# A three-stage kernel: scratch columns for the squares, the prologue's orders rewritten, a rounding put ahead of a search round, and the flags in another PSUM bank

## The chip, the cores and the metric

The kernel runs on one core of a Trainium2 chip. The metric is the device time of one execution in microseconds (us), lower being better. TensorE (PE) multiplies matrices, VectorE (DVE), ScalarE (ACT) and GpSimd (POOL) work elementwise, SyncE (SP) only issues DMAs here; each works through its own queue in order, and semaphores order them against each other.

## The reference

2048 rows of 512 numbers go through three residual stages: x + 0.5 ffn(norm(x)), then x + attn(norm(x)), then x + 0.5 ffn(norm(x)).

```python
def ffn(x, A, B, Wr):                      # stages 1 and 3
    scores = x @ Wr.T                      # 64 of them a row
    top_vals, top_idx = top_k(scores, 16)
    G = scatter(softmax(top_vals))         # 0 elsewhere
    h = einsum('nd,krd->nkr', x, A)        # 64 groups of 16
    return einsum('nkr,kdr->nd', h * G[:, :, None], B) * 2.0

def attn(x, w_gate, w_up, w_down):         # stage 2, inner width 1376
    s = silu(x @ w_gate.T)
    s[the 688 smallest of |s| in each row] = 0
    return (s * (x @ w_up.T)) @ w_down.T
```

All is float32, so each product is made of three float16 products: both factors are split into a high and a low half, and hi*hi, lo*hi and hi*lo are summed.

## The kernel before

There are 16 tiles of 128 rows. A tile passes stage 1 (`experts(1, t)`: 64 scores and 1024 columns of A; `choose`, `exps`, `route` and `apply_route`: the 16 largest and their weights; `p_to_hi` and `p_to_lo`: the product's halves; `turn_p`: both halves transposed by DMA; `combine`: the product with B; `add_ffn`), stage 2 and stage 3, which is as stage 1. In stage 2 `gates`, `tanh` and `silu` make the gate, `magnitude` its absolute values and their sum, and `aim` a first guess at the threshold. Seven rounds follow: `count` on ScalarE counts how many magnitudes lie above the threshold (a sign with a sum), and `search` on GpSimd moves the threshold by four small instructions (L407 to L411). `select` on VectorE takes the exact value from the last few, and writes a flag if the threshold was too far off; `sum_flags` sums it over the partitions with a matmul of ones (L599), and `check` reads the sum and runs a slow exact search if it isn't zero. `mask`, `ups`, `gated`, `v_to_hi`, `v_to_lo`, `turn_v`, `down` and `add_down` finish the stage.

All orders are written out by hand, one list for each engine. Eleven steady tiles (`tile(d)`, `FULL` = 11) work on stage 3 of tile d, on the second half of stage 2 of d+1, on the first half of d+2, and on stage 1 of d+5. Ahead of them lies the prologue, which loads and prepares the weights, and behind them a tail.

PSUM has eight banks: `DOWN` = 0 takes the product of `down` (and in the prologue turned rows and sums of squares), `COMB` = 1 that of `combine`, 2 to 4 the wide products, 5 and 6 A's, and `SCORE` = 7 the scores; before, the flags' sum lies in column 64 of bank 7. So `sum_flags` waits until the scores ahead of it are read, and the next `experts` waits for `flag_read`.

A weight matrix is prepared in pieces. It lands in the stage `mem`; `square` on ScalarE (L681) writes its squares in bfloat16 to scratch columns; `norms` on TensorE (L492) sums them with a matrix of ones; `make_scale` on VectorE makes a power of two of the largest; `split_hi` (L688, ScalarE) and `split_lo` (L892, VectorE) write the halves. The matrices are `MR` (scores, 1 piece), `MA` (4), `MB` (4), `MG` (gate, 4), `MU` (up, 4) and `MD` (down, 6). The stage is shared: `w_u` is loaded over what `w_a` and `w_b` used, once `w_b` is split, and `w_d` over `w_g`, once that is split; both loads are issued by GpSimd. The scratch columns before are two buffers that take turns, so a square waits for the sums of the one before the last:

```python
if turn >= 2:
    act.wait_ge(norm_summed, turn - 1)
```

A norm needs GpSimd for its root: `norm_stats` on VectorE, `rstd` on GpSimd (L389, L393), `norm_apply` on VectorE (L915), then `x_to_hi` (ScalarE), `x_to_lo` (VectorE, L923) and `turn_x`, a DMA transpose.

Of the kernel before, what the change touches and what calls it, by code (L numbers as in the profile page):

```python
# [13 lines left out]
P = 128  # L14
# [56 lines left out]
def build(nc, x, w_r, w_a, w_b, w_g, w_u, w_d, out):  # L71
# [35 lines left out]
    with ExitStack() as ctx:  # L107
# [153 lines left out]
        def _(sp):  # L261
# [17 lines left out]
            def turn_x(j, t):  # L279
                sp.wait_ge(x_hi_ready[j], t + 1)  # L280
                sp.wait_ge(x_lo_ready[j], t + 1)
                if j == 2:
                    if t == 1:

                        sp.wait_ge(norm_summed, pieces_before(MD) + len(MD.pieces))
# [56 lines left out]
            turn_x(2, 1)  # L342
            turn_x(1, 4)
# [32 lines left out]
        def _(pool):  # L376
# [77 lines left out]
            searches(0, 0, 1, 2)  # L454
            rstd(2, 2)
            searches(0, 3, 4, 5)
# [20 lines left out]
        def _(pe):  # L477
# [6 lines left out]
            def norms(m, first=0, end=None):  # L484

                for n, (c, k, rows) in list(enumerate(m.pieces))[first:end]:
                    pe.wait_ge(squared, pieces_before(m) + n + 1)
                    sq = squares(m, n)
                    for q in range(k):
                        for b in m.blocks:  # L490
                            o, w = b * BANK, min(BANK, m.width - b * BANK)
                            mm = pe.matmul(bank(m.bank, w), ones[0:rows, :],  # L492
                                           sq[0:rows, q * m.width + o:q * m.width + o + w],
# [18 lines left out]
            def experts(j, t, fresh=False, norms_of=None):  # L512
# [15 lines left out]
                mm.then_inc(scored, 1)  # L528
                if k:
                    pe.wait_ge(routed_ready, k)  # L530
# [6 lines left out]
                else:  # L537
                    for o in range(2):
# [3 lines left out]
                        if o == 0 and norms_of is not None:  # L542
                            norms(norms_of)
# [36 lines left out]
            def down(t):  # L580
                if t == 0:
                    split_done(MD, IC - 1)
                else:
                    pe.wait_ge(x2_ready, t)
                pe.wait_ge(vt_hi_loaded, 16 * (t + 1))
# [36 lines left out]
            pe.wait_ge(scale_made, 3)  # L622
# [15 lines left out]
            gates(1)  # L638
# [658 lines left out]
```

## Time and profile before

| | us |
|---|---|
| median of three runs (lowest, highest) | 831.62 (831.41, 834.43) |
| the profiled execution | 832.65 |
| its span | 830.8 |

| engine | busy us | share of the span |
|---|---|---|
| PE (matmul) | 725.8 | 87% |
| DVE | 480.1 | 58% |
| ACT | 359.8 | 43% |
| POOL | 212.9 | 26% |

Busy time is the time in which at least one instruction of the engine ran. In the page's 40 slices PE shows low digits in the first seven and in the last two, and is at 9 tenths nearly everywhere between. A wait in the trace is the idle time of an engine ahead of an instruction, with what ended it; "issue" stands for an end that the profile doesn't show.

### The profile page before, as it was taken

What the parts mean: (1) busy time and instruction counts of PE and PEld (TensorE: products, weight loads), DVE (VectorE), ACT (ScalarE), POOL (GpSimd) and SP (SyncE); (2) the same over time, 40 slices, a digit from 0 to 9 for tenths busy, and PEclk for the clock granted to TensorE, in tenths of its full rate; (3) what the DMA queues carried; (4) which work ended last, traced back from release to release, by engine and by line L of the source; (5) the groups of instructions that cost most, each with busy time, mean ns of one, the idle gap of its engine ahead of it and who ended that gap; (6) DMA issues with size and microseconds to landing.
All of it is one profiled execution on the core that took longest, in us unless ns stands there. A gap on an engine that the chain in (4) does not pass through costs nothing.

```text
span 830.8 us, 10394 instructions
## 1 busy us (share of the span) xinstructions
PE 725.8 (87%) x3674; PEld 337.4 (41%) x3679; DVE 480.1 (58%) x1015; ACT 359.8 (43%) x447; POOL 212.9 (26%) x618
## 2 busy tenths in 40 slices
PE   4676779759999999999999999999999996989684
PEld 1223334324454545444444444444445442434231
DVE  6656647446666576665747475665666553544631
ACT  5454655425253534435352625352535343446110
POOL 4013030314132323223140504141323222223100
PEclk9997889879999999999999999999999997999898
DMA  8429412315152424334243333251414140403221
GB/s 327 119 89 197 112 27 39 60 13 99 32 95 49 99 51 82 68 68 83 61 83 68 63 81 69 54 83 37 89 38 99 26 86 13 86 19 81 52 59 38
DMA packets 170524, 62.29 MB, mean 75 GB/s; under 512 B 163632, under 2 KB 163632, under 8 KB 170464
## 3 DMA queue, kind: packets, MB, share of 16 engines
q1 hardware_dynamic: 167952, 51.01, 31.3%
q0 software_dynamic: 2512, 10.55, 4.0%
q8 instruction: 29, 0.48, 0.2%
q14 instruction: 31, 0.25, 0.1%
HBM read 16.97 MB, written 4.19 MB: 25 GB/s over the span
## 4 chain that ended last, share of the span: by engine, by line
DVE 32%; POOL 19%; issue 18%; ACT 13%; PE 12%; DMA 3%; DVEq 1%; SPq 1%; POOLq 0%; ACTq 0%
ACT signs L719 9%; POOL small L411 5%; POOL small L409 4%; PE ps L480 4%; PE ps L482 4%; PE ps L481 4%; DVE mem L1007 3%; DVE small L1009 3%; POOL small L408 3%; DVE mem L1026 3%; DVE mem L987 3%; DVE mem L1087 3%; DVE stats L908 3%; POOL small L407 2%; ACT mem L737 2%
## 5 line engine op out<-in xcount | busy, mean ns | idle before, releaser
L719 ACT ACTIVATE signs<-mem,small 128x1376 bf16<-128x1376 f32 x112 | 161.4, 1441 | 144.5 <-POOL small L411 125.6
L480 PE MATMUL ps<-w_b_hi,pt_hi 128*128 128x512 f16 x256 | 97.7, 382 | 21.1 <-issue 21.1
L480 PE MATMUL ps<-w_a_hi,xt_f 128*128 128x512 f16 x256 | 101.9, 398 | 5.2 <-DVE routed L957 3.4
L481 PE MATMUL ps<-w_a_hi,xt_f 128*128 128x512 f16 x256 | 101.4, 396 | 0.0
L482 PE MATMUL ps<-w_a_lo,xt_f 128*128 128x512 f16 x256 | 101.3, 396 | 0.0
L389 POOL TENSOR_SCALAR rvar<-mv 128x1 f32<-128x1 f32 x48 | 11.4, 237 | 351.1 <-DVE mv L909 350.1
L481 PE MATMUL ps<-w_b_hi,pt_lo 128*128 128x512 f16 x256 | 97.7, 382 | 0.0
L482 PE MATMUL ps<-w_b_lo,pt_hi 128*128 128x512 f16 x256 | 97.5, 381 | 0.0
L967 DVE TENSOR_TENSOR p_lo<-routed,p_hi 128x1024 f16<-128x1024 f32 x32 | 39.2, 1225 | 85.5 <-ACT p_hi L714 75.8
L480 PE MATMUL ps<-w_u_hi,xt 128*128 128x512 f16 (+1 forms) x192 | 70.3, 366 | 6.7 <-DVE mem L987 6.7
L480 PE MATMUL ps<-w_g_hi,xt 128*128 128x512 f16 (+1 forms) x192 | 70.9, 369 | 3.9 <-issue 3.9
L481 PE MATMUL ps<-w_g_hi,xt 128*128 128x512 f16 (+1 forms) x192 | 70.8, 369 | 0.0
L482 PE MATMUL ps<-w_g_lo,xt 128*128 128x512 f16 (+1 forms) x192 | 70.5, 367 | 0.0
L481 PE MATMUL ps<-w_u_hi,xt 128*128 128x512 f16 (+1 forms) x192 | 70.1, 365 | 0.0
L482 PE MATMUL ps<-w_u_lo,xt 128*128 128x512 f16 (+1 forms) x192 | 70.1, 365 | 0.0
L703 ACT ACTIVATE mem<-mem 128x512 f16<-128x512 f32 x16 | 10.1, 629 | 134.3 <-DVE mem L915 134.3
L480 PE MATMUL ps<-w_d_hi,mem 128*128 128x512 f16 x176 | 66.7, 379 | 1.7 <-DMA mem<-mem 1.7
L481 PE MATMUL ps<-w_d_hi,mem 128*128 128x512 f16 x176 | 66.7, 379 | 0.0
L482 PE MATMUL ps<-w_d_lo,mem 128*128 128x512 f16 x176 | 66.7, 379 | 0.0
L923 DVE TENSOR_TENSOR halves<-normed,halves 128x512 f16<-128x512 f32 x30 | 20.8, 692 | 65.2 <-ACT halves L703 65.2
L407 POOL TENSOR_SCALAR small<-small 128x1 f32<-128x1 f32 x96 | 21.4, 223 | 131.1 <-ACT signs L719 129.7
L411 POOL TENSOR_SCALAR small<-small,steps 128x1 f32<-128x1 f32 x96 | 47.9, 499 | 10.2
(130 smaller groups left out, 1218.6 us busy)
## 6 DMA issues: line engine op xcount, KB each, us to landing
x<-x SPq DMA_DIRECT2D x14, 256.0 KB, 3.0
out<-x SPq DMA_DIRECT2D x14, 256.0 KB, 2.4
mem<-w_g POOLq DMA_DIRECT2D x4, 688.0 KB, 8.2
mem<-w_u POOLq DMA_DIRECT2D x4, 688.0 KB, 7.4
mem<-w_d POOLq DMA_DIRECT2D x5, 512.0 KB, 12.0
mem<-w_a SPq DMA_DIRECT2D x4, 512.0 KB, 6.2
mem<-w_b POOLq DMA_DIRECT2D x4, 512.0 KB, 6.5
pt_hi<-p_hi SPq DMA_TRANSPOSE x32, 3.2
```

The costliest lines, as they stand in the source:

```text
L407: link(pool.tensor_scalar(off, bal, -7.0, None, ALU.add))
L408: link(pool.tensor_scalar(far, off, off, 7.5 ** 2, ALU.mult, ALU.is_gt))
L409: link(pool.tensor_tensor(move, off, far, ALU.mult))
L411: pool.tensor_scalar(thr, move, steps[:, n:n + 1], thr, ALU.mult, ALU.add).then_inc(thr_ready, 1)
L480: pe.matmul(dst, x_hi, w_hi, start=start, stop=False)
L481: pe.matmul(dst, x_lo, w_hi, start=False, stop=False)
L482: return pe.matmul(dst, x_hi, w_lo, start=False, stop=stop)
L719: act.activation(signs[:, :], mags[t % 2], ACT.Sign, bias=thr, scale=-1.0, accum_out=bal).then_inc(counted, 1)
L908: link(dve.bn_stats(stats[j][:, :], slot(t)))
L967: dve.tensor_tensor(p_lo[:, :], routed[:, :], p_hi[:, :], ALU.subtract).then_inc(p_lo_ready, 1)
L987: dve.scalar_tensor_tensor(out=gate, in0=gate, scalar=1.0, in1=bank(WIDE, I), op0=ALU.add, op1=ALU.mult).then_inc(gate_ready, 1)
L1007: link(dve.scalar_tensor_tensor(out=masked[:, 0:I], in0=mag, scalar=thr, in1=mag, op0=ALU.is_le, op1=ALU.mult))
```

## The change

1. Each matrix gets scratch columns for the squares of all its pieces, in places that are filled only later: `MR` in `signs`, `MA` and `MB` in `w_u`'s halves, `MG` and `MU` in `w_d`'s halves, `MD` in the stage's first columns. The wait of `square` on `norm_summed` goes, and so does `turn_x(2, 1)`'s; the first square of `MD` waits until `MU` is split. The zeros of `w_d`'s last rows are written after `silu(0)`.
2. In the prologue, the orders of SyncE, TensorE, ScalarE and VectorE are rewritten: squares run earlier and in pairs, `norms` of `MB` and `MG` stand between the scores and the wait for `routed`, `experts(1, 4)` ahead of `ups(0)`, `turn_x(2, 0)` ahead of `turn_p(2)`, `gated(0)` behind the scale of `MD`. On GpSimd `rstd(2, 2)` comes one search round earlier.
3. In the steady tile, `p_to_hi` of stage 3 runs ahead of `count` 5 instead of behind it.
4. The flags' sum lies in bank `DOWN`. `sum_flags` waits for `add_down` of the tile before, `down` waits for the flag's reading, and no `experts` does. In the last tiles it stands behind `gates`.

```diff
         def squares(m, n):
-            one = xt_2[1].rearrange("p c t -> p (c t)") if m is MD else signs[:, :]
-            two = keep[:, :]
-            return [one, two][(pieces_before(m) + n) % 2].bitcast(BF16)
+            c, k, rows = m.pieces[n]
+            place = {"r": signs[:, :], "a": hi["u"], "b": lo["u"], "g": hi["d"], "u": lo["d"],
+                     "d": mem[:, 0:2 * IPAD]}[m.name]
+            if m.name in "abgu":
+                place = place.rearrange("p c w -> p (c w)")
+            return place.bitcast(BF16)[0:rows, c * m.width:(c + k) * m.width]
...
             load_x(2)
+            load_x(3)
             turn_x(1, 2)
-            load_x(3)
+            load_x(4)
             turn_p(0)
-            load_x(4)
-            turn_p(1)
-            turn_x(1, 3)
             load_x(5)
             load_x(6)
+            turn_x(1, 3)
+            turn_p(1)
+            turn_x(2, 0)
             turn_p(2)
-            turn_x(2, 0)
+            turn_x(1, 4)
             turn_p(3)
...
                 mm.then_inc(scored, 1)
+                if norms_of is not None:
+                    norms(norms_of)
                 if k:
                     pe.wait_ge(routed_ready, k)
...
-            def sum_flags(t, k):
-                pe.wait_ge(scores_read, k + 1)
+            def sum_flags(t):
+                if t:
+                    pe.wait_ge(x2_ready, t)
                 pe.wait_ge(flag_ready, t + 1)
-                pe.matmul(bank(SCORE, 1, KE), ones[:, :], flag[:, 0:1], start=True, stop=True
+                pe.matmul(bank(DOWN, 1), ones[:, :], flag[:, 0:1], start=True, stop=True
...
                 if d:
                     combine(3, d - 1)
-                sum_flags(d + 1, number[1, d + LEAD] - 1)
+                sum_flags(d + 1)
                 gates(d + 2)
-                pe.wait_ge(flag_read, d + 2)
                 experts(1, d + LEAD)
...
+            pe.wait_ge(scale_made, 4)
             norms(MU)
-            pe.wait_ge(scale_made, 4)
             gates(0, fresh=True)
+            combine(1, 2)
+            experts(1, 4)
+            ups(0, fresh=True)
             pe.wait_ge(scale_made, 5)
-            norms(MD, 0, 2)
-            combine(1, 2)
-            norms(MD, 2, 4)
-            ups(0, fresh=True)
-            norms(MD, 4, 6)
-            experts(1, 4)
+            norms(MD)
             combine(1, 3)
             gates(1)
...
-                if turn >= 2:
-                    act.wait_ge(norm_summed, turn - 1)
...
                 exps(number[3, d])
-                counts(d + 2, 4, 5)
+                count(d + 2, 4)
                 p_to_hi(number[3, d])
-                count(d + 2, 6)
+                counts(d + 2, 5, 6)
```

## Rows read from the trace of the kernel before

**Rows 1.** The page, part 4: the chain that ended last, by engine.
```profile
DVE 32%; POOL 19%; issue 18%; ACT 13%; PE 12%; DMA 3%; DVEq 1%; SPq 1%; POOLq 0%; ACTq 0%
```

**Rows 2.** Busy time by stretch; columns PE, PEld, DVE, ACT, POOL, granted clock, DMA, GB/s.
```profile
27.30:148.20 120.90, 87.61 (x399) 38.83 (x404) 73.92 (x154) 62.62 (x67) 20.47 (x53) 0.87 0.39 90
172.70:652.60 479.90, 462.10 (x2443) 219.89 (x2444) 296.61 (x631) 210.10 (x272) 139.00 (x403) 0.99 0.36 68
```

**Rows 3.** Timeline of PE, a steady tile: start, duration, what, idle before.
```profile
570.15 0.38 PE L480 MATMUL ps<-w_b_hi,pt_hi 128*128 128x512 f16 x1 [1.51 <-issue]
...
575.36 0.38 PE L480 MATMUL ps<-w_g_hi,xt 128*128 128x512 f16 x1
...
582.33 0.19 PE L480 MATMUL ps<-w_r_hi,xt_f 128*128 128x64 f16 x1
```

**Rows 4.** Waits of DVE, 27.3 to 148.2: us in total, times, longest.
```profile
DVE p_lo L967 <- DMA pt_lo<-p_lo: 9.7, 1, 9.7
DVE w_b_lo L892 <- ACT w_b_hi L688: 8.6, 1, 8.6
DVE halves L923 <- ACT halves L703: 7.2, 2, 5.8
...
DVE normed L915 <- POOL rvar L393: 2.7, 3, 1.0
```

**Rows 5.** Timeline of DVE, prologue: the low halves of B, and G's last.
```profile
50.61 4.87 DVE L892 SCALAR_TENSOR_TENSOR w_b_lo<-mem,small,w_b_hi 128x1024 f16<-128x1024 f32 x4 [8.62 <-ACT w_b_hi L688]
...
70.36 1.64 DVE L892 SCALAR_TENSOR_TENSOR w_g_lo<-mem,small,w_g_hi 128x1376 f16<-128x1376 f32 x1
```

**Rows 6.** The tile pt_lo, 0 to 180: issue to landing of its transposes.
```profile
DMA to landing us min/median/max: 3.2/3.6/14.2
```

**Rows 7.** Timeline of ACT, a steady tile: rounds 4, 5 and 6 (L719), `p_to_hi`.
```profile
604.22 1.44 ACT L719 ACTIVATE signs<-mem,small 128x1376 bf16<-128x1376 f32 x1 [0.89 <-POOL small L411]
...
607.20 1.44 ACT L719 ACTIVATE signs<-mem,small 128x1376 bf16<-128x1376 f32 x1 [1.44 <-POOL small L411]
...
608.64 1.04 ACT L714 ACTIVATE p_hi<-routed 128x1024 f16<-128x1024 f32 x1
611.18 1.44 ACT L719 ACTIVATE signs<-mem,small 128x1376 bf16<-128x1376 f32 x1 [1.50 <-POOL small L411]
```

**Rows 8.** Timeline of DVE, the same tile: `add_down`, `choose`, `apply_route` and `p_to_lo`.
```profile
574.65 0.75 DVE L980 SCALAR_TENSOR_TENSOR x<-ps,small,x 128x512 f32<-128x512 f32 x1
...
584.20 0.22 DVE L935 COPY scores<-ps 128x64 f32<-128x64 f32 x1
...
604.42 1.22 DVE L957 TENSOR_TENSOR routed<-ps,weight 128x1024 f32<-128x1024 f32 x1
609.71 1.23 DVE L967 TENSOR_TENSOR p_lo<-routed,p_hi 128x1024 f16<-128x1024 f32 x1 [4.06 <-ACT p_hi L714]
```

**Rows 9.** Timelines of POOL and DVE: L411 alone, and beside a VectorE instruction.
```profile
606.82 0.34 POOL L411 TENSOR_SCALAR small<-small,steps 128x1 f32<-128x1 f32 x1
...
609.80 1.35 POOL L411 TENSOR_SCALAR small<-small,steps 128x1 f32<-128x1 f32 x1
...
154.41 1.81 POOL L411 TENSOR_SCALAR small<-small,steps 128x1 f32<-128x1 f32 x1
...
154.46 1.63 DVE L1087 TENSOR_TENSOR mem<-mem 128x1408 f16<-128x1408 f32 x1 [3.01 <-ACT mem L737]
```

**Rows 10.** Timelines of PE and DVE, the first steady tile.
```profile
177.32 0.16 PE L599 MATMUL ps<-flag,ones 128*128 128x1 bf16 x1 [10.21 <-DVE flag L1020]
...
186.67 0.19 PE L480 MATMUL ps<-w_r_hi,xt_f 128*128 128x64 f16 x1
...
178.77 0.75 DVE L980 SCALAR_TENSOR_TENSOR x<-ps,small,x 128x512 f32<-128x512 f32 x1
...
187.39 0.22 DVE L935 COPY scores<-ps 128x64 f32<-128x64 f32 x1
```

**Rows 11.** Timeline of PE, tail: the start of `ups(15)`.
```profile
747.50 0.39 PE L480 MATMUL ps<-w_u_hi,xt 128*128 128x512 f16 x1 [1.84 <-DVE mem L987]
```

More of the change, by code:

```diff
@@ L676, in square @@
                 c, k, rows = m.pieces[n]
-                turn = pieces_before(m) + n
                 act.wait_ge(w_loaded[m.name][n], 16)
-                if turn >= 2:
-                    act.wait_ge(norm_summed, turn - 1)
-                act.activation(
-                    squares(m, n)[0:rows, 0:k * m.width].rearrange("p (c w) -> p c w", c=k),
-                    staged(m, c, k, rows), ACT.Square).then_inc(squared, 1)
+                if m is MD and n == 0:
+                    wait_low(act, MU, len(MU.pieces) - 1)
+                act.activation(squares(m, n).rearrange("p (c w) -> p c w", c=k),
+                               staged(m, c, k, rows), ACT.Square).then_inc(squared, 1)
             def split_hi(m, n):
@@ L771, in _ @@
                 split_hi(MA, n)
+            square(MB, 0)
+            square(MB, 1)
             x_to_hi(1, 2)
+            square(MB, 2)
+            square(MB, 3)
             exps(0)
-            for n in range(len(MB.pieces)):
-                square(MB, n)
+            square(MG, 0)
+            square(MG, 1)
             p_to_hi(0)
-            square(MG, 0)
+            square(MG, 2)
+            square(MG, 3)
             exps(1)
-            for n in range(1, len(MG.pieces)):
-                square(MG, n)
             for n in range(len(MB.pieces)):
                 split_hi(MB, n)
+            x_to_hi(1, 3)
             p_to_hi(1)
-            x_to_hi(1, 3)
+            split_hi(MG, 0)
+            split_hi(MG, 1)
             exps(2)
-            for n in range(len(MG.pieces)):
-                split_hi(MG, n)
+            split_hi(MG, 2)
+            split_hi(MG, 3)
             p_to_hi(2)
@@ L790, in _ @@
             exps(3)
-            square(MU, 0)
-            square(MU, 1)
-            square(MU, 2)
+            for n in range(len(MU.pieces)):
+                square(MU, n)
             p_to_hi(3)
-            square(MU, 3)
-            square(MD, 0)
-            square(MD, 1)
+            x_to_hi(1, 4)
             for n in range(len(MU.pieces)):
@@ L800, in _ @@
             tanh(0)
-            square(MD, 2)
-            square(MD, 3)
             x_to_hi(2, 1)
+            square(MD, 0)
+            square(MD, 1)
             magnitude(0)
             count(0, 0)
+            square(MD, 2)
+            exps(4)
+            count(0, 1)
+            square(MD, 3)
+            count(0, 2)
+            p_to_hi(4)
             square(MD, 4)
-            count(0, 1)
+            count(0, 3)
             square(MD, 5)
-            x_to_hi(1, 4)
-            count(0, 2)
-            count(0, 3)
-            exps(4)
             count(0, 4)
-            p_to_hi(4)
             x_to_hi(2, 2)
@@ L1138, in _ @@
             turned_to_lo(1)
+            split_lo(MA, 0)
             norm_stats(1, 2)
-            split_all(MA)
+            for n in range(1, len(MA.pieces)):
+                split_lo(MA, n)
             norm_apply(1, 2)
@@ L1153, in _ @@
             norm_apply(1, 3)
-            split_all(MB)
             make_scale(MG)
             make_unscale(unscale_g, "g", 38)
+            split_lo(MB, 0)
+            x_to_lo(1, 3)
+            split_lo(MB, 1)
+            choose(2)
+            split_lo(MB, 2)
+            split_lo(MB, 3)
             p_to_lo(1)
-            x_to_lo(1, 3)
-            choose(2)
             route(2)
@@ L1162, in _ @@
             split_lo(MG, 0)
-            split_lo(MG, 1)
             add_ffn(1, 0)
             norm_stats(2, 0)
+            split_lo(MG, 1)
+            norm_apply(2, 0)
             split_lo(MG, 2)
-            norm_apply(2, 0)
+            x_to_lo(2, 0)
             split_lo(MG, 3)
+            choose(3)
             p_to_lo(2)
-            x_to_lo(2, 0)
-            choose(3)
             route(3)
             apply_route(3)
-            p_to_lo(3)
             norm_stats(1, 4)
@@ L1178, in _ @@
             norm_stats(2, 1)
+            x_to_lo(1, 4)
             make_scale(MU)
             norm_apply(2, 1)
+            p_to_lo(3)
             split_all(MU)
@@ L1198, in _ @@
             x_to_lo(2, 2)
+            make_scale(MD)
+            make_unscale(unscale_m, "gud", -83)
+            link(dve.memset(masked[:, I:IPAD], 0.0))
+            gated(0)
             add_ffn(1, 3)
@@ L1201, in _ @@
             norm_apply(1, 5)
+            split_lo(MD, 0)
             select(0)
             mask(0)
-            split_all(MD)
+            for n in range(1, len(MD.pieces)):
+                split_lo(MD, n)
             x_to_lo(1, 5)
```

47 lines of the change are left out of this document (16 added, 31 removed).

## The prediction, made before the changed kernel had run

> **What bounds the kernel now.** I read the page's chain first, then the busy time by stage, then one tile of the steady loop engine by engine, then the waits of the prologue. The profiled execution took 832.65 us with a span of 830.8, so 1.85 us lie around the span; the median of the three runs is 831.62, 1.0 below it. I work in the profiled execution's frame and take 1.0 off at the end.
>
> The chain that ends last is mostly VectorE, GpSimd and ScalarE, with TensorE at 12% [rows 1], although the page has TensorE as the busiest engine. The stages say how both can hold. In the eleven steady tiles (172.7 to 652.6) TensorE is busy 462.1 of 479.9 us [rows 2], with some 1.5 us idle in each tile, in front of `combine` of stage 3 [rows 3]. That wait is slack, not the limit: a tile takes about 44.1 us because of a ring that goes round once a tile and in which no matmul is late: `v_to_hi`, `v_to_lo`, `choose`, `silu`, `magnitude`, seven `count`/`search` rounds, `select`, `mask`, `add_down`, norm of stage 3, `check`, `v_to_hi`. In the prologue from 27.3 to 148.2 (the start of `silu(1)`, with which the ring begins to turn) VectorE is busy 73.92 of 120.9 us and TensorE 87.61 [rows 2]; neither is full. VectorE's queue there is a fixed list of work, the same in both kernels, and what decides is the 47.0 us in which it isn't busy. Its largest waits are 9.7 for a landing of `pt_lo`, 8.6 for `split_hi(MB)`, 7.2 for `x_to_hi`; each trip over GpSimd for a root costs up to 1.0 [rows 4].
>
> **The change part by part.**
>
> *Squares in columns of their own, and the prologue's orders.* Before, two scratch buffers took turns, so that `square` n waited for the sums of n-2, and those sums stood behind `experts(1,0)` and in the middle of `experts(1,1)` and `experts(1,2)`, which wait for routing. That is what the 8.6 is: the scale of B comes late, and the one of G later. In the new order I walk the queues; an engine's step costs the distance to the next start on it. ScalarE squares B right behind `split_hi(MA)` and in two pairs, the last one done at 25.1; the sums now go ahead of TensorE's wait for `routed`, so they are there at 27.3, when VectorE is done with `apply_route(0)`. Its list from there: scale and unscale of B 2.4, `choose` 1.5, `p_to_lo` 1.1, `norm_stats` 0.8, `route` and `apply_route` 1.9, `norm_apply` 0.5, scale and unscale of G 2.2, that is 37.8; then four pieces of `w_b_lo` at 1.2 with `x_to_lo` 0.6 and a `choose` 1.5 between, that is 44.8 for the last of B, 55.4 now; then `p_to_lo`, `route` and `apply_route` 3.0, `add_ffn` and `norm_stats` 1.6, four pieces of `w_g_lo` at 1.6, `norm_apply` and `x_to_lo` 1.1 and a trip for a root, that is 57.6 for the last of G, 72.0 now [rows 5]. What TensorE owes to these steps (`experts(1,1)` 5.3 from 27.5, `experts(1,2)` 5.3 from 35.3) is done earlier each time. What VectorE still waits for:
> - three trips for a root that nothing covers, (2,0), (1,4) and (1,5), at 1.0 each, and `rstd(2,2)`, which now stands behind the search of round 1: 2.1. Together 5;
> - `x_to_lo(1,4)` and `p_to_lo(3)` need `p_hi(2)` and `p_lo(2)` turned. These two transposes are issued at about 57.4 and 60.3, and `w_d` is issued at 57.7, so they share the engines with it. The median landing of `pt_lo` is 3.6 us, the worst 14.2 beside a weight load [rows 6]. I take 9 to 12, nearer the worst since the load is the same one: 3 us of waits at VectorE's place in its queue;
> - `exps(4)` behind a count and a square: 1;
> - `p_to_lo(4)` behind round 2 and then `x_to_lo(2,2)` behind rounds 3 and 4. A round is 2.98 [rows 7]; 1.3 and 5.4 are left after the work that lies between.
>
> That is 16 us. With it go the seams between instructions that no wait explains, about 4 us, as now. So 20 stand against 47.0, and the two memsets of `w_d`'s last rows, which were under the first load and now follow `silu(0)`, add 0.7. Gain 47.0 - 20 - 0.7 = 26.3; the walk by start times instead of by sum puts `silu(1)` at 120.0, which is 28.2. I take 27. Bounds: if the transposes land in the median time, nothing of the 3 stays and a few of the trips are covered, 31; if both land as late as 14.2 and the gates that need `xt_2` too, which moves every later step, 18. What is late next is VectorE itself: from 27.3 it is then busy about four fifths of the time.
>
> *Orders of the DMA queues.* SyncE issues `x` of tile 3 with the first ones and `turn_x(2,0)` ahead of `turn_p(2)`. Behind `turn_x(2,0)` now wait both halves of `turn_p(2)`, hence the hi half at 57.4 though `p_hi(2)` is ready at 49; this is in the 3 us above. GpSimd issues `w_u` when `w_b_lo` is done, 44.9 for 55.8, and `w_d` at 57.7 for 72.3; landing ends some 9 and 14 us later, ahead of the squares that read them (58 and 80). The squares of `w_d` lie on the stage of `w_u`, so they wait for its last split, 79.5, and `gated(0)` in turn waits for the scale of `w_d`; in the walk that wait is the 5.4.
>
> *p_to_hi one round earlier.* In the steady tile ScalarE now has a gap of 1.5 us after round 4 as after every other, and `routed` is ready 1.42 after that round's start (604.42 + 1.22 against 604.22) [rows 7, 8]. So `p_hi` goes at 605.67 for 608.64, `p_lo` 3.0 earlier, and `combine` loses its 1.5 us wait. But two things take the gain. First, the clash moves along: before, `p_lo` at 609.71 stretches GpSimd's L411 at 609.80 from 0.34 to 1.35 [rows 8, 9], which is why round 6 starts 3.98 after round 5 and not 2.98 [rows 7]. After, `p_lo` starts at 605.67 + 1.04 + 0.03 = 606.74, again just ahead of L411 at 606.82. Round 5 comes 1.0 later, round 6 when it did. Zero on the ring.
>
> *Flags in the down bank.* `sum_flags(d+1)` now waits for `add_down(d)`, and `gates(d+2)` and all of TensorE's tile are queued behind it. `add_down` ends at 574.65 + 0.75 = 575.40 [rows 8]; today the gates start at 575.36 [rows 3]. With the wait, a weight load and the small matmul they start at about 575.6. So the 1.5 us just changes its place, from before `combine` to before the flag, and the gates are 0.2 later. Who waits for them: `choose` at 584.20 [rows 8] needs the scores, now ready at 582.9 [rows 3]; 1.0 us of slack remain, `apply_route` has 0.6. Cost zero. The exception is tile 0, where the wait is on the path now: TensorE stands 10.2 us for the flag, starts the gates right behind the flag's matmul of 177.32, at the low clock, and reaches the scores at 186.67; `choose` follows at 187.39, without slack [rows 10]. `add_down(0)` ends at 178.77 + 0.75 = 179.52, so the gates start at about 179.7 and everything is 2.2 later. Cost 2.2, once.
>
> *The tail.* TensorE doesn't wait for flags ahead of the gates of tile 14, but the ring does, and `experts(3,12)` needs a transpose that lands at 712.4 in any case: nothing. Later the short wait of 1.84 for `silu(15)` [rows 11] shrinks with the one before it and its slow start may go, while `experts(3,14)` starts ahead of `check` and TensorE then stands longer before the last `down`. I put both at 0, with 2 us to either side.
>
> **The sum.** 832.65 - 27 + 2.2 = 807.9; less 1.0 for the median: 806.9 us (3.0% off the median).
>
> **Rivals.**
> - *The clash is missed.* The margin between `p_lo` and L411 is 0.07 us. If L411 comes first, it takes 0.34 and round 5 isn't late: 1.0 in each of 11 tiles, 795.9. Against: `v_to_lo`, started at 154.46, stretched an L411 that the profile starts at 154.41 [rows 9], so the window in which VectorE wins reaches past GpSimd's start. 9%. The Trainium skill's page "SBUF — State Buffer", section "SBUF: two separate sides", says that of a VectorE instruction with two inputs in SBUF and a GpSimd instruction the one that starts first has the shared ports to its end, and the other blocks. By that rule the order alone decides, and the gain of this rival follows as soon as GpSimd is first; the row at 154.41 differs, with GpSimd first by 0.05 us and blocked all the same.
> - *The prologue's gain sticks half way.* The transposes next to `w_d` land late and `gates(0)` with them, so that `silu(0)` slips by 5 to 9: 812 to 816. For it: 14.2 [rows 6]. 17%.
> - *The clock falls at the new wait.* Today TensorE stands 1.5 us a tile at full clock [rows 3]; in tile 0, after 10.2 us, the gates took 9.2 us instead of 7.0 [rows 3, 10]. If the stand ahead of the gates brings the low clock, the gates cost 2.2 more, 1.0 of it slack: 1.2 in each of 10 tiles, 819. It ends on the other side from the point where a fall costs more than 1.0 + 25/10 = 3.5 us per tile, as two falls a tile would (4.4): 806.9 + 34 = 841. Against: the same length of idling leaves the granted clock of the stage at 0.99 today, with tile 0's low stretch in it [rows 2]. 3% for 819, 3% for slower.
> - *The change doesn't do what it says*: the walk misses a wait of VectorE as long as those it removes, and `silu(1)` is where it was: 834 on paper, 830 to 835. 3%.
>
> **How the numbers follow.** The forecast has 65% (800 to 812). The rival at 795.9 has 9, the half gain 17, the rest 9. Range: from 795 up to 817, which leaves out the slow and the unchanged cases, half of the missed clash and walks that are off in both ways. A measurement of this kernel tells about 0.5% (4 us) from no change. Faster 0.93, within 0.5% 0.03, slower 0.04.
>
> **What would show it.** Right: `silu(1)` near 120 and `select(1)` near 145; VectorE idle about 20 of the stretch; steady tiles of 44.1 us as before, with TensorE's 1.5 us now ahead of the flag's matmul and the stretched L411 one round earlier. Wrong: a tile of 43.1 (clash missed), PEclk under 1.00 in the steady tiles, or `p_lo(3)` waiting for a transpose beyond 75.

## The result and the profile after

The changed kernel takes 808.3 us (median of four runs, 808.08 to 809.25), the kernel before 832.74 beside it (four runs, 831.41 to 834.43): a ratio of 0.9708, 95% interval 0.9684 to 0.9731. The profiled execution took 808.51, its span is 806.7.

The chain of the page after is made up as before [rows 1]; the next view is the busy time by stretch, for the prologue up to `silu(1)` and for the eleven steady tiles (columns as in rows 2).

```profile
DVE 32%; POOL 19%; issue 17%; PE 14%; ACT 12%; DMA 3%; DVEq 1%; SPq 0%; POOLq 0%; ACTq 0%
...
27.30:119.57 92.27, 80.62 (x398) 36.68 (x396) 74.46 (x156) 59.00 (x64) 21.89 (x53) 0.96 0.48 115
146.30:626.20 479.90, 462.21 (x2440) 220.18 (x2441) 296.31 (x632) 210.34 (x271) 140.47 (x401) 0.99 0.37 68
```

VectorE's list of the prologue is 74.46 us for 73.92 [rows 2], but it takes 92.27 instead of 120.92: the idle time fell from 47.0 to 17.8. The waits of VectorE in that stretch (us in total, times, longest) answer to rows 4, and its timeline answers to rows 5; the last line of it is `silu(1)`, which stood at 148.22.

```profile
DVE halves L915 <- ACT halves L692: 5.3, 1, 5.3
DVE normed L907 <- POOL rvar L393: 4.9, 4, 2.2
DVE p_lo L959 <- DMA pt_lo<-p_lo: 2.2, 1, 2.2
DVE p_lo L959 <- ACT p_hi L703: 1.0, 1, 1.0
DVE chosen L940 <- ACT expd L696: 0.9, 1, 0.9
```

```profile
42.70 2.48 DVE L884 SCALAR_TENSOR_TENSOR w_b_lo<-mem,small,w_b_hi 128x1024 f16<-128x1024 f32 x2
...
56.27 1.64 DVE L884 SCALAR_TENSOR_TENSOR w_g_lo<-mem,small,w_g_hi 128x1376 f16<-128x1376 f32 x1
...
119.57 1.58 DVE L979 SCALAR_TENSOR_TENSOR mem<-mem,ps 128x1376 f32<-128x1376 f32 x1
```

The steady tile, timelines of ScalarE (rounds 4, 5, 6 at L708, `p_to_hi` at L703), GpSimd (L411) and VectorE; they answer to rows 7 to 9. Round 5 now starts 4.00 after round 4, round 6 2.99 after round 5.

```profile
578.30 1.44 ACT L708 ACTIVATE signs<-mem,small 128x1376 bf16<-128x1376 f32 x1 [0.90 <-POOL small L411]
...
579.74 1.06 ACT L703 ACTIVATE p_hi<-routed 128x1024 f16<-128x1024 f32 x1
582.30 1.44 ACT L708 ACTIVATE signs<-mem,small 128x1376 bf16<-128x1376 f32 x1 [1.50 <-POOL small L411]
...
585.29 1.44 ACT L708 ACTIVATE signs<-mem,small 128x1376 bf16<-128x1376 f32 x1 [1.45 <-POOL small L411]
```

```profile
580.91 1.36 POOL L411 TENSOR_SCALAR small<-small,steps 128x1 f32<-128x1 f32 x1
584.92 0.34 POOL L411 TENSOR_SCALAR small<-small,steps 128x1 f32<-128x1 f32 x1
```

```profile
578.49 1.22 DVE L949 TENSOR_TENSOR routed<-ps,weight 128x1024 f32<-128x1024 f32 x1
580.83 1.22 DVE L959 TENSOR_TENSOR p_lo<-routed,p_hi 128x1024 f16<-128x1024 f32 x1 [1.12 <-ACT p_hi L703]
```

The flags' sum (TensorE, L598) in tile 0 and in a steady tile, with VectorE's `add_down(0)` and `choose`; they answer to rows 3 and 10.

```profile
150.97 0.19 PE L598 MATMUL ps<-flag,ones 128*128 128x1 bf16 x1 [12.54 <-DVE x L972]
...
593.73 0.18 PE L598 MATMUL ps<-flag,ones 128*128 128x1 bf16 x1 [1.48 <-DVE x L972]
```

```profile
150.16 0.75 DVE L972 SCALAR_TENSOR_TENSOR x<-ps,small,x 128x512 f32<-128x512 f32 x1
...
160.91 0.23 DVE L927 COPY scores<-ps 128x64 f32<-128x64 f32 x1 [2.04 <-PE ps L482]
```

And the tail: TensorE's flags' sum of tile 12 behind `gates(13)`, `ups(15)` (as rows 11) and the last `down`, then VectorE's `check` and `v_to_lo` of tile 12.

```profile
643.27 0.17 PE L598 MATMUL ps<-flag,ones 128*128 128x1 bf16 x1
...
723.91 0.39 PE L480 MATMUL ps<-w_u_hi,xt 128*128 128x512 f16 x1 [1.83 <-DVE mem L979]
...
765.47 0.38 PE L480 MATMUL ps<-w_d_hi,mem 128*128 128x512 f16 x1 [2.40 <-DMA mem<-mem]
```

```profile
643.51 0.16 DVE L1068 CAST ints<-ps 128x1 int32<-128x1 f32 x1 [1.86 <-PE ps L598]
...
646.24 1.62 DVE L1079 TENSOR_TENSOR mem<-mem 128x1408 f16<-128x1408 f32 x1 [1.44 <-ACT mem L726]
```

One measure serves all kernels below: the instruction at the end of `select` that writes `flag`, once a tile. From the timelines of VectorE I took its start in each tile; the table has the first, some distances between neighbours, and what is left behind the last one up to the end of the span (us).

| kernel | flag(0) | 0 to 1 | 1 to 2 | 9 to 10 | 12 to 13 | 13 to 14 | 14 to 15 | rest | span |
|---|---|---|---|---|---|---|---|---|---|
| before | 139.16 | 37.80 | 43.21 | 44.19 | 42.35 | 42.35 | 34.55 | 51.1 | 830.8 |
| changed | 111.70 | 36.65 | 45.42 | 44.24 | 44.54 | 42.42 | 32.87 | 52.3 | 806.7 |
| swap_only | 136.63 | 37.86 | 43.29 | 44.26 | 42.43 | 42.43 | 34.44 | 52.1 | 830.2 |
| flags_only | 139.26 | 37.79 | 45.19 | 44.18 | 45.29 | 42.36 | 32.87 | 53.1 | 836.1 |
| flags_back | 113.11 | 36.60 | 43.32 | 44.25 | 42.37 | 42.36 | 34.55 | 51.1 | 804.1 |
| flag_order | 113.20 | 36.66 | 43.28 | 44.25 | 42.43 | 41.54 | 32.95 | 53.1 | 804.1 |
| columns_only | 124.81 | 37.84 | 43.25 | 44.23 | 42.42 | 42.41 | 34.56 | 50.8 | 816.8 |
| columns_norms | 124.03 | 37.80 | 43.21 | 44.18 | 42.38 | 42.37 | 34.55 | 52.3 | 816.9 |
| norms_back | 124.69 | 36.64 | 45.31 | 44.26 | 44.55 | 42.40 | 32.88 | 53.0 | 820.4 |
| squares_wait | 129.75 | 36.66 | 45.00 | 44.26 | 44.54 | 41.42 | 33.25 | 52.3 | 823.9 |
| lo_before | 141.07 | 37.81 | 42.53 | 43.51 | 42.68 | 42.37 | 34.55 | 50.9 | 825.5 |
| lo_after_search | 113.28 | 36.60 | 44.24 | 43.20 | 45.36 | 42.35 | 32.87 | 50.9 | 795.8 |
| best1 | 113.86 | 36.61 | 41.50 | 42.50 | 43.46 | 42.37 | 32.87 | 50.9 | 785.8 |
| best2 | 112.56 | 36.60 | 41.50 | 42.51 | 42.47 | 41.48 | 32.87 | 52.8 | 784.5 |

The first column varies between kernels whose prologues are the same, by 4.4 us for the old one (136.63 to 141.07) and by 2.2 for the new one (111.70 to 113.86). The distances hardly vary but for 13 to 14, which is 0.9 shorter in three kernels (see flag_order and best2), and the rest behind the last flag lies anywhere from 50.8 to 53.1. The changed kernel's 808.3 was measured at another time than the medians below, between which the kernel before went from 832.74 up to 835.18. So a difference of a few us to the changed kernel is read from the distances, not from the medians.

### The profile page after: what moved, and what is told of

Same layout as the page of the kernel before. It is cut to its first block, busy times and chain, and to the rows that moved or that the text cites. A ratio compares the mean times of both kernels' runs of the same rounds, so it can differ in the third digit from the quotient of the medians.

```text
span 806.7 us, 10393 instructions
## 1 busy us (share of the span) xinstructions
PE 720.3 (89%) x3679; PEld 336.8 (42%) x3679; DVE 480.1 (60%) x1015; ACT 360.5 (45%) x447; POOL 215.3 (27%) x618
## 4 chain that ended last, share of the span: by engine, by line
DVE 32%; POOL 19%; issue 17%; PE 14%; ACT 12%; DMA 3%; DVEq 1%; SPq 0%; POOLq 0%; ACTq 0%
ACT signs L708 9%; POOL small L411 5%; PE ps L480 5%; PE ps L481 5%; PE ps L482 4%; POOL small L409 4%; DVE mem L999 3%; POOL small L408 3%; DVE small L1001 3%; DVE mem L979 3%; DVE mem L1018 3%; DVE stats L900 2%; DVE mem L1079 2%; POOL small L407 2%; ACT mem L726 2%
## 5 line engine op out<-in xcount | busy, mean ns | idle before, releaser
L708 ACT ACTIVATE signs<-mem,small 128x1376 bf16<-128x1376 f32 x112 | 161.5, 1442 | 146.7 <-POOL small L411 127.8
L480 PE MATMUL ps<-w_a_hi,xt_f 128*128 128x512 f16 x256 | 99.5, 389 | 2.2 <-DVE w_a_lo L884 1.2
L481 PE MATMUL ps<-w_a_hi,xt_f 128*128 128x512 f16 x256 | 99.4, 388 | 0.0
L482 PE MATMUL ps<-w_a_lo,xt_f 128*128 128x512 f16 x256 | 99.0, 387 | 0.0
L480 PE MATMUL ps<-w_u_hi,xt 128*128 128x512 f16 (+1 forms) x192 | 69.3, 361 | 6.6 <-DVE mem L979 6.6
L481 PE MATMUL ps<-w_u_hi,xt 128*128 128x512 f16 (+1 forms) x192 | 69.1, 360 | 0.0
L999 DVE SCALAR_TENSOR_TENSOR mem<-mem,small 128x1376 f32<-128x1376 f32 x16 | 26.4, 1651 | 71.0 <-ACT signs L708 70.9
```

The source lines that it names most:

```text
L480: pe.matmul(dst, x_hi, w_hi, start=start, stop=False)
L481: pe.matmul(dst, x_lo, w_hi, start=False, stop=False)
L482: return pe.matmul(dst, x_hi, w_lo, start=False, stop=stop)
L708: act.activation(signs[:, :], mags[t % 2], ACT.Sign, bias=thr, scale=-1.0, accum_out=bal).then_inc(counted, 1)
L999: link(dve.scalar_tensor_tensor(out=masked[:, 0:I], in0=mag, scalar=thr, in1=mag, op0=ALU.is_le, op1=ALU.mult))
```

## The experiments

### The parts alone: the swap (swap_only)

```diff
                 exps(number[3, d])
-                counts(d + 2, 4, 5)
+                count(d + 2, 4)
                 p_to_hi(number[3, d])
-                count(d + 2, 6)
+                counts(d + 2, 5, 6)
```

> The kernel before with part 3 alone: p_to_hi of stage 3 ahead of round 5 in the steady tiles. Theory (the clash of p_to_lo with GpSimd's L411 only moves one round earlier, and the ring round which a tile's work goes binds, not TensorE's 1.5 us wait): 0 against the kernel before, within 1 us; round 5 starts 4.0 after round 4 and round 6 starts 3.0 after round 5, where before it was 3.0 and 4.0, and a tile stays at 44.1. Rival 1 (the clash is missed): 1.0 less in each of 11 tiles, 11 us faster. Rival 2 (the 1.5 us wait ahead of combine was on the path): up to 1.5 in each tile, 16 us faster. Rival 3 (both rounds late): 11 us slower.

Measured: 833.62 (12 runs, 829.82 to 836.84) beside 833.99 (23 runs); ratio 0.999, interval 0.9962 to 1.0017. The tiles stay at 44.26, round 5 starts 4.02 after round 4 and round 6 2.99 after round 5. The swap alone is worth nothing, as forecast.

### The parts alone: the flags (flags_only)

The edit is part 4 of the diff on the kernel before.

> The kernel before with part 4 alone: the flags' sum in bank DOWN, in tile 0 behind add_down(0), in the two tiles behind the steady ones behind the gates. Theory: +2.2 in tile 0 (the gates start behind the flag instead of behind the add_down that is 2.2 earlier... that is, TensorE's whole tile is queued behind the new wait and choose has no slack there), 0 in the other steady tiles, +2.2 where sum_flags stands behind the gates of tile 13, because check waits for it: 4 to 5 us slower than before. Rival 1 (only the two waits' sum is hidden by slack): 0. Rival 2 (the new wait in front of the gates costs the 1.5 us that it stands in every tile, because combine's wait of 1.5 stays in this kernel): +10 to +16.

Measured: 838.86 (12 runs) beside 833.99; ratio 1.0057, 1.0029 to 1.0085, so 4.9 us slower. The distances say where: 1 to 2 grows by 1.98, 12 to 13 by 2.94, 14 to 15 shrinks by 1.68, the other steady tiles don't move. So both rivals fall, and the theory stands for its two terms, with 2.94 for the second 2.2. The agreement of the sum is in part luck: the theory had neither the 1.68 nor the rest, which is 2.0 longer in this profile. (Its condition in tile 0 in plain words: the gates used to start right behind the flag, 2.2 ahead of the end of `add_down(0)`, and are now held until then.)

### The flags taken back (flags_back)

The edit is part 4 in reverse, on the changed kernel.

> The changed kernel with part 4 taken back: flags' sum in column 64 of bank 7 and in its old places, the rest as changed. Theory: the 2.2 of tile 0 and the 2.2 of tile 13's check come back, so 3.5 to 4.5 us less than the changed kernel, 804 to 805; select of tile 0 at about 187.3 instead of 189.5. Rival (the loss in the tail belongs to the earlier end of the steady tiles, not to sum_flags' place): 2.2 less, 806. Rival 2 (bank DOWN buys something in the steady tiles, since experts no longer waits for the flag's reading): no less than 808.

Measured: 804.81 (5 runs) beside 833.99; ratio 0.9651, 0.9616 to 0.9686; 3.5 below the changed kernel's 808.3. Tile 0 gives back 2.10, 12 to 13 gives back 2.17, and 14 to 15 loses 1.68, because `ups(15)` starts slowly again (720.81 to 729.64, 8.8 us for the 7.1 of the changed kernel). The first rival falls, since the two losses come back one by one, and so does the second.

### The order in TensorE's queue (flag_order)

In `tile(d)`, and in the loop behind the steady tiles:

```diff
                 if d:
                     combine(3, d - 1)
-                sum_flags(d + 1)
+                    sum_flags(d + 1)
                 gates(d + 2)
+                if d == 0:
+                    sum_flags(1)
...
+                if d == FULL:
+                    sum_flags(d + 1)
                 gates(d + 2)
-                sum_flags(d + 1)
+                if d > FULL:
+                    sum_flags(d + 1)
```

> The changed kernel, the flags' sum still in bank DOWN, but in tile 0 behind the gates and in tile 13's place ahead of them. Theory (the order in TensorE's queue is the whole loss, 2.2 in tile 0 and 2.2 at tile 13's check, and the late ups(15) keeps its full clock, which the kernel with part 4 taken back lost): 4.4 us less than the changed kernel, 804, and level with that kernel or up to 1.7 better. Rival (the tail's 2.2 comes from add_down and not from the queue): 806.

Measured: 803.18 (6 runs, 802.26 to 805.88) beside 835.0; ratio 0.9623, 0.9594 to 0.9651. The distances 43.28, 42.43 and 32.95 are the better ones of both kernels in each column. The bank is innocent: the place in the queue cost 2.14 and 2.11 us, 4.25 for a forecast 4.4. The medians are 5.1 apart. The distance 13 to 14, which neither side named, is 0.88 shorter: GpSimd's L409, which took 1.00 beside `p_lo` there in the changed kernel (698.98), took 0.19 in this one, because `p_lo` came 0.5 later. With the same order in TensorE's queue, best1 has that clash again (1.05), so it is a chance of a small margin and not the worth of the edit.

### The columns alone (columns_only)

```diff
-            one = xt_2[1].rearrange("p c t -> p (c t)") if m is MD else signs[:, :]
-            two = keep[:, :]
-            return [one, two][(pieces_before(m) + n) % 2].bitcast(BF16)
+            if m is MD:
+                one = xt_2[1].rearrange("p c t -> p (c t)")
+                return [one, keep[:, :]][(pieces_before(m) + n) % 2].bitcast(BF16)
+            c, k, rows = m.pieces[n]
+            place = {"r": signs[:, :], "a": hi["u"], "b": lo["u"], "g": hi["d"], "u": lo["d"]}[m.name]
...
-                if turn >= 2:
+                if m is MD:
                     act.wait_ge(norm_summed, turn - 1)
```

> The kernel before with the scratch columns alone (those of MR, MA, MB, MG and MU; MD keeps its two buffers and their wait), all orders as before, the two memsets behind silu(0). Theory (columns and orders are worth something only together: the sums of B stand in TensorE's queue behind experts that wait for routing whatever the columns are): at most the 2 to 4 us of the squares that were held up, 829 to 832 with the memsets' 0.7 against it. Rival (the columns alone end VectorE's wait of 8.6 for w_b_hi, and with it a third of the gain): silu(1) 8 us or more earlier, 824 or less.

Measured: 819.62 (4 runs, 818.58 to 825.1) beside 835.0; ratio 0.984, 0.9796 to 0.9883: 13 us faster by the ratio, 15.4 between the medians. The rival is right and the theory wrong: `silu(1)` starts at 133.87, 14.35 earlier. The two lines are VectorE's low halves of B in this kernel (for 50.61 and a wait of 8.62 in rows 5) and its start on G's scale.

```profile
37.60 4.87 DVE L897 SCALAR_TENSOR_TENSOR w_b_lo<-mem,small,w_b_hi 128x1024 f16<-128x1024 f32 x4
...
44.10 0.69 DVE L873 TENSOR_REDUCE small<-ps 128x1 f32<-128x512 f32 x1 [1.63 <-PE ps L497]
```

What the buffers' turns held up was not the squares of B alone. In the kernel before, ScalarE stood 8.91 us for a sum ahead of the third square of G, and `split_hi(MB)` is queued behind that.

```profile
46.95 1.35 ACT L681 ACTIVATE keep<-mem 128x1376 bf16<-128x1376 f32 x1 [8.91 <-PE ps L492]
48.21 1.33 ACT L681 ACTIVATE signs<-mem 128x1376 bf16<-128x1376 f32 x1
49.45 4.25 ACT L688 ACTIVATE w_b_hi<-mem,small 128x1024 f16<-128x1024 f32 x4
```

### The wait put back under the new orders (squares_wait)

```diff
+                if pieces_before(m) + n >= 2:
+                    act.wait_ge(norm_summed, pieces_before(m) + n - 1)
```

> The changed kernel with the wait of square on the sums of the one before the last put back; scratch columns and all orders stay as changed. Theory (VectorE's waits for w_b_hi and w_g_hi were the worth of the columns: squares run ahead of the norms, and a scale is there as soon as TensorE has summed): the squares of B wait for sums that stand behind experts(1,1) and routing again, B's scale comes some 5 to 9 us later, and silu(1) starts at 125 to 130 instead of 119.6; 6 to 10 us slower than changed. Rival (the reordering of TensorE's and ScalarE's queues is the whole 28 us, since norms now stand ahead of the wait for routed in any case): within 1.5 us of the changed kernel.

Measured: 823.79 (4 runs, 820.86 to 825.72) beside 833.99; ratio 0.9863, 0.9819 to 0.9906: 15.5 above the changed kernel, `silu(1)` at 137.62, 18.05 later. The theory had the sign and the mechanism but half of the size. B is late by 7.2 (52.36 for the 45.18 at which its last low half ends), which it said; what it missed is that `exps` stand behind squares in ScalarE's new order, so that `route` waits too. The longest of these waits, 9.6, ends at 104.27, behind a square of `MD` that ScalarE starts at 102.77 after 8.63 us of waiting for a sum. VectorE's waits in the prologue, of this kernel:

```profile
DVE chosen L942 <- ACT expd L698: 16.2, 3, 9.6
```

### The place of the sums (norms_back)

```diff
                 mm.then_inc(scored, 1)
-                if norms_of is not None:
-                    norms(norms_of)
                 if k:
                     pe.wait_ge(routed_ready, k)
...
+                        if o == 0 and norms_of is not None:
+                            norms(norms_of)
```

> The changed kernel with the sums of MB and MG back between the two halves of experts(1, 1) and (1, 2), behind the wait for routed; columns and all other orders as changed. Theory (by the walk, B's scale is ready as VectorE ends apply_route(0), and it would now come a half of the experts, 2.7, and the sums later): 3 to 4 of wait at B's scale, as much again at G's if nothing takes it up, silu(1) at 123 to 127 for 119.6, 812 to 816. Rival (the columns alone did it, and this place is worth nothing, since VectorE's 16 us of other waits absorb it): within 1.5 us of the changed kernel.

Measured: 820.58 (4 runs, 818.41 to 822.26) beside 835.18; ratio 0.9816, 0.9784 to 0.9848: 12.3 above the changed kernel, `silu(1)` at 132.56. The waits are at the two scales, as the theory has it, but 6.3 and 6.4 each for its 3 to 4. VectorE in this kernel:

```profile
34.16 0.69 DVE L860 TENSOR_REDUCE small<-ps 128x1 f32<-128x512 f32 x1 [6.27 <-PE ps L492]
...
48.92 0.69 DVE L860 TENSOR_REDUCE small<-ps 128x1 f32<-128x512 f32 x1 [6.42 <-PE ps L492]
```

The first of them is the half of the experts, 4.45 (27.95 to 32.40), and the sums, 1.67. The half took 4.45 and not 2.7, because eight of its twelve matmuls took 0.61 to 0.63 for 0.38, after TensorE had stood 2.29 us for `routed`; the granted clock of that half is 0.62. The second is alike: idle 4.64, a granted clock of 0.57 from 42.0 to 46.0, and 4.29 for the half. At 0.38 each the half takes 2.6 in this trace. So the slow stretch is 1.7 to 1.9 of each wait, and the queue that the theory named is the rest, 4.4 to 4.7 for its 3 to 4.

```profile
27.95 0.39 PE L480 MATMUL ps<-w_a_hi,xt_f 128*128 128x512 f16 x1 [2.29 <-DVE routed L949]
...
28.61 0.61 PE L480 MATMUL ps<-w_a_hi,xt_f 128*128 128x512 f16 x1
29.01 0.63 PE L481 MATMUL ps<-w_a_hi,xt_f 128*128 128x512 f16 x1
```

### Columns and place of the sums, in the old orders (columns_norms)

The edit is that of columns_only, with `norms(norms_of)` ahead of the wait for `routed`.

> The kernel before with the scratch columns alone, and besides them only the sums of MB and MG moved ahead of TensorE's wait for routed; all other orders as before. Runs so far put silu(1) at 148.22 before, 133.87 with the columns alone, 119.57 with all of the change, and 132.56 with all but this place of the sums. Theory (the place of the sums is worth 13 wherever it is made): silu(1) at 120 to 122, 806 to 808. Rival (it is worth that much only where VectorE's scale of B stands ahead of its routing, since the old order of VectorE takes the scale later and covers most of the wait, all but 1.6): silu(1) at 131 to 133, 815 to 819, so that the columns bring one half and the other half needs the rewritten orders as one.

Measured: 818.06 (4 runs, 816.93 to 820.03) beside 834.42; ratio 0.9807, 0.9785 to 0.9829, and `silu(1)` at 133.10. The rival is right. In the old order VectorE comes to B's scale at 32.95, behind `p_to_lo(0)`, `norm_stats(1, 3)` and `choose(1)`, where the sums are there anyway; in the new one at 27.68. So the place of the sums is worth 0.8 us in the old orders and 13.0 in the new ones, and the rest of the orders without that place 1.3 (133.87 to 132.56). The 0.8 and the 1.3 are less than equal prologues differ by, so they may be nothing; the 13.0 is not. The last 14 us of the prologue belong to the orders as a set: one that asks for the scale early, and one that has it ready.

### The clash taken away (lo_after_search)

```diff
-            def p_to_lo(k):
+            def p_to_lo(k, after=None):
...
+                if after is not None:
+                    dve.wait_ge(thr_ready, after)
...
                 apply_route(k3)
-                p_to_lo(k3)
+                p_to_lo(k3, ROUNDS * (d + 2) + 6)
```

> The changed kernel with one wait more: in the steady tiles p_to_lo of stage 3 waits until GpSimd's search of round 4 is done, some 0.45 us. So L411 runs alone, 0.34 instead of 1.34. Theory (the clash at a margin of 0.07 us costs the ring 1.0 in each tile, and TensorE, busy 42.7 of 44.2, doesn't bind yet): 1.0 in each of 11 tiles less, 797, tiles of 43.2. Rival 1 (the clash comes back at the next instruction, L407 of round 5 or at another VectorE instruction): within 2 us of the changed kernel. Rival 2 (TensorE binds first, as combine waits for the later p_lo): 4 to 6 us less.

Measured: 797.66 (6 runs, 795.79 to 800.64) beside 835.0; ratio 0.9562, 0.953 to 0.9593: 10.6 below the changed kernel. GpSimd's L411 and VectorE's `p_to_lo` in a steady tile:

```profile
572.76 0.34 POOL L411 TENSOR_SCALAR small<-small,steps 128x1 f32<-128x1 f32 x1
```

```profile
573.23 1.23 DVE L961 TENSOR_TENSOR p_lo<-routed,p_hi 128x1024 f16<-128x1024 f32 x1 [1.65 <-POOL small L411]
```

Tiles of 43.20 for 44.24, while VectorE's idle time ahead of `p_lo` grows from 1.12 to 1.65, by 0.53 us. Both rivals fall. 0.8 comes back at 12 to 13 (45.36 for 44.54).

### The same wait in the kernel before (lo_before)

The edit is the same, with `+ 7` for `+ 6`, since `p_hi` is there one round later.

> The kernel before, p_hi still behind round 5, with the wait alone: p_to_lo of stage 3 waits until the search of round 5 is done, so that L411 runs alone there too. It tells what part 3 was worth beside the clash. Theory (the clash was 1.0 of the ring before as well, and the later p_lo still finds 1.0 of slack at choose and 0.6 at apply_route): 1.0 in each of 11 tiles less, 821 to 822, that is as much as the same wait brought the changed kernel, and moving p_to_hi is worth nothing by itself. Rival (TensorE's wait ahead of combine grows by the 0.45 and takes the slack): 826 or more, and part 3 is what lets the wait pay.

Measured: 827.19 (6 runs, 825.4 to 829.03) beside 835.18; ratio 0.9906, 0.988 to 0.9932. The tile is 43.51, 0.68 less than before and not 1.04. Against the kernel before it is 8.0 less, where the theory had 11 and the rival at most 7. The clash was there, and two thirds of it come back. The rival's reason isn't the one: TensorE's idle time ahead of `combine` doesn't grow, it is down from 1.5 to 0.85, and what `apply_route` waits for TensorE (0.2 to 0.5 in most tiles) doesn't show in the tile. The last third is lost in VectorE's own queue, between this kernel's round 6 (ScalarE) and `add_ffn` and `select` (VectorE):

```profile
606.12 1.44 ACT L719 ACTIVATE signs<-mem,small 128x1376 bf16<-128x1376 f32 x1 [0.50 <-POOL small L411]
```

```profile
607.36 0.74 DVE L976 SCALAR_TENSOR_TENSOR x<-ps,small,x 128x512 f32<-128x512 f32 x1
608.02 1.64 DVE L1009 SCALAR_TENSOR_TENSOR mem<-mem,small 128x1376 f32<-128x1376 f32 x1
```

In the kernel before, `select` waits 1.15 for round 6 and starts 1.57 after that round's start (612.75 against 611.18). Here it stands behind the later `p_lo` and `add_ffn`, doesn't wait for the round, and starts 1.90 after it: 0.33 of the 1.01 that L411 gives back. With `p_lo` one round earlier, as in lo_after_search, `select` still waits 2.56 for round 6. So the swap, worth nothing alone, is worth some 0.3 a tile (43.51 against the 43.20 of lo_after_search) once the clash is gone.

### Both, and the flags in order (best1, then best2)

The edits are those of flag_order and lo_after_search, and for stage 1 `p_to_lo(k1, ROUNDS * (d + 2) + 2)`, behind the search of round 0.

> The changed kernel with flag_order's places, the wait of the kernel before it in this call, and the same for p_to_lo of stage 1 against the search of round 0, where L409 takes 1.20 instead of 0.19. Theory (each clash on the ring is worth its whole stretch until TensorE is full): ring 42.2 to 42.4, TensorE at 42.65 a tile binds, some 1.5 a tile less than changed and 4.4 for the flags: 786 to 790. Rival (waits on VectorE push its own queue, gated and choose, past their slack): 793 or more.

Measured: 787.51 (6 runs, 786.16 to 789.52) beside 835.0; ratio 0.9436, 0.9407 to 0.9466. Tiles of 42.50, in which TensorE has no wait any more: it is what binds now, as the theory has it. The wait for stage 1 takes away a second clash, which was in every steady tile of the changed kernel and of the one before: GpSimd's L409 beside stage 1's `p_lo` (1.20 for 0.19).

Behind the steady tiles, `p_to_lo(k3, ROUNDS * (d + 2) + 2)` on top of that:

> The kernel best1 with the wait on the search of round 0 also in the two tiles behind the steady ones, where L409 takes 1.20 and 1.05 beside p_to_lo. Theory: those tiles have no full TensorE behind them, so the ring takes it all, 0.8 to 1.0 in each of the two, 785.5 to 786. Rival (the transposes and TensorE's last products set these tiles): the same as best1.

Measured: 785.33 (6 runs, 784.0 to 787.73) beside 835.18; ratio 0.9404, 0.9379 to 0.9429. The distances 12 to 13 and 13 to 14 go from 43.46 and 42.37 to 42.47 and 41.48, 1.9 together. TensorE's waits of this kernel from 142 to 567, its first ten steady tiles, are two, both in tile 0; its busy time in that stretch and GpSimd's L409 and L411 in one tile, all short, stand below. A third clash is left, and costs nothing while TensorE is full: in the same tile GpSimd's L408 at 553.49 takes 0.77 beside `x_to_lo`, which starts at 553.40.

```profile
PE ps L598 <- DVE x L979: 5.5, 1, 5.5
PE ps L480 <- DVE mem L986: 3.1, 1, 3.1
```

```profile
142.00:567.00 425.00, 416.33 (x2202) 199.02 (x2201) 274.56 (x579) 193.37 (x250) 118.97 (x374) 0.99 0.37 71
```

```profile
550.64 0.19 POOL L409 TENSOR_TENSOR small<-small 128x1 f32<-128x1 f32 x1
550.94 0.34 POOL L411 TENSOR_SCALAR small<-small,steps 128x1 f32<-128x1 f32 x1
...
563.68 0.19 POOL L409 TENSOR_TENSOR small<-small 128x1 f32<-128x1 f32 x1
563.97 0.34 POOL L411 TENSOR_SCALAR small<-small,steps 128x1 f32<-128x1 f32 x1
```

This is 23 us, 2.8%, below the changed kernel by the medians; the ratios to the kernel before are 0.9404 and 0.9708.

## Why the prediction was right, and where it wasn't

The forecast was 806.9 with a range of 795 to 817; measured were 808.3.

**The prologue: right, for the reasons given.** The sum put 20 us of idle time on VectorE, the trace has 17.8. Term by term: trips for a root 5, measured 4.9 (with 2.1 for `rstd(2,2)`, 2.25 in the trace); transposes beside `w_d` 3, measured 2.2 (the slowest landing of `pt_lo` 11.0, for a forecast 9 to 12); `exps` 1, measured 0.9; `p_to_lo(4)` 1.3, measured 1.0; `x_to_lo(2,2)` 5.4, measured 5.3; seams 4, measured 3.5. The last of B is done at 45.2 for a forecast 44.8, the last of G at 57.9 for 57.6, `silu(1)` starts at 119.57 for 120.0. The gain is 28.65; the 27 between sum and walk was the more cautious choice, and the walk alone (28.2) the better one.

What the prediction said of the cause was too narrow. It put the 8.6 us wait down to the sums' place and the two buffers together. The runs part them: the buffers alone 14.35, the new orders on top of them 14.3, and of the orders the sums' place counts for 13.0 with the rest of the new orders and for 0.8 without. The columns were enough to end the wait of 8.6 with the sums in their old place.

**Tile 0: right.** The gates start behind the flag at 150.97, `choose` comes at 160.91 behind a wait of 2.04 for TensorE. Distance 1 to 2 is 2.21 longer, for 2.2 forecast.

**The steady tiles: right.** 44.24 a tile for 44.19. The clash moved as forecast: L411 at 580.91 takes 1.36, just behind `p_lo` at 580.83, and the idle time of TensorE stands ahead of the flag (1.48) and not ahead of `combine`. The rival of the missed clash is dead here, and its price, 1.0 a tile, was right all the same: lo_after_search gets 10.6. The rival of the falling clock is dead too: the gates behind the new wait (593.91 to 601.00) run at a granted clock of 1.00. The 0.99 of the whole stretch, though under the 1.00 that the prediction set as a sign, is also that of the kernel before, with tile 0's slow gates in it. What the prediction didn't see is the second clash of each tile (L409, see best1); it is the same in both kernels and so no part of the difference. On the chip's side the rows now say more than they did. In the steady tiles VectorE starts first, by 0.08 us, and GpSimd's instruction ends 0.22 after it. Where GpSimd starts first, it takes 0.34: by 0.47 in lo_after_search, and by 0.20 at 696.61 in flag_order, ahead of `p_lo` at 696.81. The Trainium skill's page "SBUF — State Buffer", section "SBUF: two separate sides", has whichever of the two starts first hold the shared ports for its whole instruction; these rows agree with it, and the one of rows 9 where GpSimd, first by 0.05, was stretched to 1.81 doesn't. The changed kernel has that one again, with L411 at 125.78 for 1.79 and `v_to_lo` at 125.81.

**The tail: the step that failed.** The prediction put the flags' new place in the tail at 0, with the words that TensorE doesn't wait for flags ahead of the gates of tile 14 and that `experts(3,12)` needs a transpose in any case. It looked at tile 14 and overlooked tile 13, the first one behind the steady tiles. There `sum_flags` moved behind `gates(13)`, whose matmuls end at 643.44, while `check` of tile 12 and the `v_to_lo` behind it on VectorE are on the ring; `check` waits 1.86 for the sum. 12 to 13 grows by 2.19. Part of that comes back as forecast: `ups(15)` goes at a granted clock of 1.00 for 0.81 (7.1 us, 723.91 to 731.05, for 8.8), 1.68. The rest behind the last flag is 1.2 longer. In this trace `experts(3,14)` is done earlier, TensorE stands 2.40 for the transpose (1.24 before) and `down(15)` takes 9.0 us at a granted clock of 0.81, where it took 7.3 before:

```profile
765.47:774.44 8.97, 8.97 (x34) 3.75 (x35) 1.23 (x1) 0.02 (x1) 0.00 (x0) 0.81 0.31 60
```

But the rest lies between 50.8 and 53.1 over all kernels and doesn't follow the flags' place alone (best1 50.9, best2 52.8, with the same code there), so how much of the 1.2 is the change's stays open. Net the tail costs 1.8 (2.19 - 1.68 + 1.2 + 0.1), inside the 2 that the prediction allowed.

**The sum** in the profiled frame: -28.6 + 2.2 + 0.5 (nine steady tiles, within their variation between kernels) + 1.8 is -24.1; forecast were -24.8. Of the 1.0 that I took off for the median only 0.2 was there: the changed kernel's profiled run is 808.51, its median 808.3. These two small misses are the 1.4 us between forecast and result. That they are so small is partly luck: the prologue gave 1.6 more than the 27 that was taken, the tiles and the tail took 2.3 that stood at 0, and equal prologues differ by as much.

## What to carry to other kernels

A buffer that is reused makes its writer wait, and everything queued behind the writer: count the whole queue, not the step that the buffer serves. An early demand and an early supply are worth something only together, so test the parts of a reordering in the old and in the new order before one of them gets the credit. And where two engines clashed at a margin of hundredths of a us, moving the work only moved the clash; 0.5 us more of waiting on the engine with slack removed 1.0 on the one without.

## What the hardware showed that wasn't expected

- 0.53 us more of waiting on VectorE in each tile makes the tile 1.04 shorter. One instruction of GpSimd on a single column (L411, 0.34) takes 1.36 when it starts within 0.08 us behind VectorE's 128x1024 one.
- TensorE, idle for 2.29 us in the prologue, ran matmuls of 512 columns at 0.38 to 0.40 three times and then eight of them at 0.61 to 0.63 (norms_back, 27.95 to 32.0, granted clock 0.62). Idle for about 1.5 ahead of the flag in a steady tile of the changed kernel, it kept 0.38 (granted clock 1.00). The slow stretches are 1.7 to 1.9 of each of norms_back's waits of 6.3 and 6.4.
- Identical prologues end up to 4.4 us apart from run to run (`flag(0)` from 136.63 to 141.07), while identical steady tiles agree within 0.1 (44.18 to 44.26 for 9 to 10 with the clash at L411).
